# A masked two-layer graph kernel: shorter constant set-up, loads in order of use, four quads ahead of the loop, last units by halves, store wait behind the final branch, and a branch hint

## What is computed

```python
N, D = 4096, 128            # x: (N, D) f32, adj: (N, N) int32, about 0.2% of it ones, diagonal 1
# layer 0, with A' = adj + I: the mask adds nan_to_num(-inf * (1 - A'))
x = layernorm(x + softmax((x @ Wq) @ (x @ Wk).T + mask, axis=1) @ (x @ Wv))
# layer 1
h = x @ W.T + b_W
e = (h @ a1)[:, None] + (h @ a2)[None, :] + b_a[0]
e = where(e > 0, e, 0.2 * e)
att = softmax(where(adj > 0, e, -9e15), axis=1)
x = layernorm(x + att @ h)
```

## Time and profile before

| | us |
|---|---|
| median of 3 runs | 276.06 |
| lowest, highest | 275.21, 276.06 |
| the profiled execution, its own time | 275.45 |
| its span | 273.6 |

### The profile page before, as it was taken

The page is one execution under the profiler, slowest core; times in us unless marked ns, Lnnn a source line. Parts: engine busy times, 40 slices in busy tenths (PEclk is TensorE's granted clock), DMA queues, the critical chain, the costliest instruction groups (busy, mean ns, idle before and its releaser), DMA issues.

```text
span 273.6 us, 3890 instructions
## 1 busy us (share of the span) xinstructions
PE 238.2 (87%) x1488; PEld 133.9 (49%) x1488; DVE 200.6 (73%) x318; ACT 147.5 (54%) x174; POOL 47.8 (17%) x68
## 2 busy tenths in 40 slices
PE   3836599999629999999999999999999999999920
PEld 3734566546224555455644545556555555544410
DVE  2392597999987777877698777786977776978080
ACT  3049864976666557664686676646866750101010
POOL 2065041555540000000022000000220000014020
PEclk9998689999968999999999999999999999999985
DMA  5999999999979999999696989898989100001101
GB/s 146 352 410 403 248 286 419 408 406 351 317 289 320 341 320 340 393 291 412 188 415 180 410 265 401 274 410 257 372 229 415 55 0 0 2 0 38 41 21 61
DMA packets 24057, 71.73 MB, mean 262 GB/s; under 512 B 5347, under 2 KB 5604, under 8 KB 24036
## 3 DMA queue, kind: packets, MB, share of 16 engines
q1 hardware_dynamic: 23748, 71.32, 73.2%
q10 hardware_dynamic: 288, 0.13, 0.2%
HBM read 69.36 MB, written 2.10 MB: 261 GB/s over the span
## 4 chain that ended last, share of the span: by engine, by line
issue 39%; PE 24%; POOL 4%; ACT 1%; DVE 1%; POOLq 0%
PE banks L791 19%; PE banks L771 3%; POOL frstd L330 2%; POOL out_sb L337 2%; PE banks L739 1%; PE banks L819 1%; ACT a L396 1%; DVE e_sb L579 1%; POOLq L236 0%; DVE out_sb L691 0%; ACT R L384 0%; ACT v_exp L372 0%; ACT cr_exp L374 0%; ACT cr_exp L376 0%; DVE frv L604 0%
## 5 line engine op out<-in xcount | busy, mean ns | idle before, releaser
L579 DVE SCALAR_TENSOR_TENSOR e_sb<-R,c_word,banks 128x1024 f32<-128x1024 f32 x128 | 159.5, 1276 | 37.4 <-PE banks L771 36.8
L791 PE MATMUL banks<-e_sb,f_parts 128*128 128x512 f16 x768 | 185.0, 389 | 0.0
L396 ACT ACTIVATE a<-a_sb 128x2048 fp8e4<-128x2048 int32 x64 | 119.8, 1904 | 66.0 <-PE banks L771 51.3
L791 PEld LDWEIGHTS banks<-e_sb,f_parts 128*128 128x128 f16 x768 | 71.8, 97 | 85.4 <-issue 2.2
L771 PEld LDWEIGHTS banks<-ident,a 128*128 128x128 f16 x512 | 34.7, 100 | 15.0 <-DVE e_sb L579 1.0
L771 PE MATMUL banks<-ident,a 128*128 128x128 f16 x512 | 40.1, 223 | 1.0 <-ACT a L396 0.5
L330 POOL TENSOR_TENSOR frstd<-frv,minus_half 128x4 f32<-128x4 f32 x8 | 8.1, 1006 | 169.8 <-DVE frv L604 169.6
L412 ACT ACTIVATE junk<-y 128x128 f32<-128x128 f32 x28 | 8.3, 297 | 22.4 <-DVE y L595 22.4
L724 PE MATMUL banks<-m0c_um,x_tr 128*128 128x130 f32 x64 | 11.2, 336 | 5.0 <-ACT xhat_st L365 5.0
L712 PE MATMUL banks<-ident,x_sb 128*128 128x128 f32 x32 | 6.5, 348 | 8.1 <-DMA x_sb<-in_x_dram 8.1
L739 PE MATMUL banks<-ident,cr_word 128*128 128x128 f32 x32 | 6.3, 330 | 7.8 <-ACT R L384 7.8
(11 more groups left out here) (96 smaller groups left out, 88.2 us busy)
## 6 DMA issues: line engine op xcount, KB each, us to landing
a_sb<-in_adj_dram SPq DMA_DIRECT2D x32, 2048.0 KB, 12.8
x_sb<-in_x_dram SPq DMA_DIRECT2D x8, 256.0 KB, 14.2
out_dram<-out_sb SPq DMA_DIRECT2D x8, 256.0 KB, 6.7
w_nat<-in_L_gnn_W_dram ACTq DMA_DIRECT2D x1, 64.0 KB, 3.3
wv<-in_L_gnn_Wv_dram ACTq DMA_DIRECT2D x1, 64.0 KB, 3.5
acol<-in_L_gnn_a_vec_dram SPq DMA_DIRECT2D x2, 0.5 KB, 3.2
bcol<-in_L_gnn_b_W_dram SPq DMA_DIRECT2D x1, 0.5 KB
brow<-in_L_gnn_b_W_dram SPq DMA_DIRECT2D x1, 0.5 KB
```

The costliest lines, as they stand in the source:

```text
L396: nc.scalar.activation(a8[:, n % 2, Q * h:Q * (h + 1), k * 512:(k + 1) * 512], a_sb[:, a % SLOTS, :].rearrange("p (r n) -> p r n", r=Q) [: ...
L579: nc.vector.scalar_tensor_tensor(out=e_sb[:, k % NE, :], in0=R[:, g % 2, :], scalar=c_word[:, 2 * t + b:2 * t + b + 1], in1=ps_code[s % NA ...
L791: ins = nc.tensor.matmul(ps_acc[g % 2][h][:, :], f[:, j, :], e_half[:, k % NE, cols, part], start=(j == 0 and n == 0), stop=(j == T - 1 an ...
```

## The change

It does nine things:

- **Constants.** A matrix `centre` (I minus 1/D) is made by POOL, so the two centring chains (reduce, scale, subtract on DVE) become matmuls against it. `m0c_um` comes from one matmul of 130 columns (`m0_t` by `centre_u`). The part that only `project` needs moves into `weights2(0)` and `weights2(1)`, behind `layer0(1)` and behind the spreads. `layer0(0)` no longer waits for `cs`, but on DVE the wait for the three bias transfers stands ahead of the copies of `centre_u` and `m0c_um`, and PE's product for `m0c_um` waits for the copy of `centre_u`; `x_turned(1)` and with it ACT's second copy stand behind `weights`.
- **Loads.** Blocks of adj have 512 columns a row (1 MB, runs of 2 KB) in 8 slots instead of 1024 columns (2 MB, runs of 4 KB) in 4. The attention vectors are loaded first, the biases behind the first two blocks.
- **Quads.** Quads 2 and 3 are turned, multiplied and kept ahead of the loop; `x_tr` has 4 buffers. From quad 2 on `divide` is done by POOL.
- **Turns.** `turn(2)` stands behind `sums(0)`, `turn(3)` and `turn(4)` behind `sums(1)`.
- **Spreads** go to slots 11 and 13 of PE; ACT's copies stay in its slots 12 and 14.
- **Group ends** (`ACC_AT` to `VARY_AT`) go one or two slots earlier, and `project` ahead of `turn` in its slot.
- **Last units.** The last three units are summed first for the left half, then for the right; the left half is copied and projected in between; the right half is copied, projected and normalised in two pieces by ACT and DVE.
- **Stores** of groups 0 and 1 are issued between the loads; SP's final wait for the stores moves behind the branch over the general code.
- **Hint.** A branch hint for PE's jump stands behind the last projections.

The core of the diff:

```diff
-    SLOTS = 4
+    LOADS = PARTS * CHUNKS * G
+    SLOTS = 8
-    AHEAD = 3
+    HALVED = 3
-    TURN, COPY, MULTIPLY, KEEP = -9, -7, -7, -5
-    STATS, DIVIDE, EXPS, PACK = -4, -2, -2, -1
-    SPREAD_AT, R_AT = 8, 12
-    ACC_AT, PROJECT_AT, FIN_AT, SQUARE_AT, VARY_AT = 5, 6, 10, 12, 14
+    TURN, COPY, MULTIPLY, KEEP = -8, -7, -6, -5
+    STATS, VARY0, EXPS, PACK = -4, -3, -2, -1
+    SPREAD_AT, R_AT = (11, 13), (12, 14)
+    ACC_AT, PROJECT_AT, FIN_AT, SQUARE_AT, VARY_AT = 4, 5, 8, 10, 12
...
+                def divide(i):
+                    pool.wait_ge(rstd_ready, i + 1)
+                    nc.gpsimd.tensor_tensor(xhat_st[:, quad_tiles(i), :], xhat_st[:, quad_tiles(i), :],
+                                            rstd[:, i % 2, :].unsqueeze(2).broadcast_to([P, Q, D + 2]),
+                                            ALU.mult).then_inc(xhat_later, 1)
...
+                step(nc.vector.tensor_tensor(m0_t[:, :], ps_m0[:, 0:D], ident[:, :], ALU.add))
+                assert done[0] == U_READY
+                dve.wait_ge(biases_loaded, 16 * 3)
...
+                assert done[0] == BB_READY
+                dve.wait_ge(pe_const, 3)
+                step(nc.vector.tensor_copy(centre_u[:, D:D + 2], ps_u[:, 2:4]))
+                dve.wait_ge(pe_const, 4)
+                step(nc.vector.tensor_copy(m0c_um[:, :], ps_m0[:, 0:D + 2]))
+                assert done[0] == M0_READY
...
+                    pe.wait_ge(vec_const, BB_READY + 1)
+                    nc.tensor.matmul(ps_m0[:, 0:D + 2], m0_t[:, :], centre_u[:, :], start=True,
                                      stop=True).then_inc(pe_const, 1)
...
-                    pe.wait_ge(acc_copied, 2 * g + 1)
-                    if last and q == 1:
-                        pe.wait_ge(acc_copied_v, 1)
...
+                def last_sums():
+
+                    units = range(S - HALVED, S)
+                    for s in units:
+                        for b in range(2):
+                            pe.wait_ge(p_ready, 2 * s + b + 1)
+                            ins = products(s, b, 0)
+                    ins.then_inc(half_done, 1)
+                    for s in units:
+                        for b in range(2):
+                            ins = products(s, b, 1)
+                        if s == S - HALVED:
+                            pe.wait_ge(acc_copied, 2 * G - 1)
+                            pe.wait_ge(y_ready, 2 * G - 2)
+                            projections(0, quad(0), range(Q)).then_inc(fin_mm, 1)
+                    ins.then_inc(half_done, 1)
...
+                last_sums()
+                to_end = pe.mark_branch_hint_location()
                 pe.wait_ge(verdict, 13)
...
-                with if_general(pe):
+                before = nc.cur_bb
+                pe.br_cond(pe.value_load(flag[0:1, 0:1]) != 0, "pe_general", "pe_end").branch_hint(to_end)
...
+                for q in range(2):
+                    sp.wait_ge(stored[q], 16 * G)
```

More of the change, by code:

```diff
@@ L221, in graph_layers, with quad_at, wait_xhat @@
         verdict_pe = sem("verdict_pe")
-        def quad_at(slot, offset):
+        def quad_at(slot, offset, first=2):
             i, odd = divmod(slot - offset, 2)
-            return i if not odd and 2 <= i < QUADS else None
+            return i if not odd and first <= i < QUADS else None
+        def wait_xhat(eng, i):
+            if i < 2:
+                eng.wait_ge(xhat_ready, i + 1)
+            else:
+                eng.wait_ge(xhat_later, i - 1)
         def group_at(slot, offset):
@@ L421, in _ @@
                 copy_xt(2)
-                codes(1)
+                copy_xt(3)
                 rows(0, 0, ps_acc[0][0])
                 rows(0, 1, ps_acc[0][1])
+                keep(2)
                 codes(2)
+                keep(3)
                 codes(3)
                 for slot in range(-2, S):
-                    if (i := quad_at(slot, COPY)) is not None and i > 2:
+                    if (i := quad_at(slot, COPY, 4)) is not None:
                         copy_xt(i)
-                    if (i := quad_at(slot, KEEP)) is not None:
+                    if (i := quad_at(slot, KEEP, 4)) is not None:
                         keep(i)
@@ L850, in _ @@
                             project(g, q, quad(2 * (g % 2)))
-                    sums(slot)
-                project(G - 1, 0, quad(0))
-                project(G - 1, 1, quad(4))
+                    if 1 < slot < S - NA:
+                        turn(slot + NA)
+                    if slot < S - HALVED:
+                        sums(slot)
+                    if slot == 0:
+                        turn(2)
+                    elif slot == 1:
+                        turn(3)
+                        turn(4)
+                last_sums()
+                to_end = pe.mark_branch_hint_location()
                 pe.wait_ge(verdict, 13)
@@ new lines, in by_rows, with by_cols @@
+                def by_rows(w):
+                    for i in range(QUADS):
+                        product(nc.tensor.matmul(bank[0][:, :], w[:, :], xhat_t[:, i * QW:(i + 1) * QW],
+                                                 start=True, stop=True))
+                def by_cols(w, bias_row):
+                    for i in range(QUADS):
+                        for q in range(Q):
+                            t = Q * i + q
+                            dst = bank[0][:, q * P:(q + 1) * P]
+                            ins = nc.tensor.matmul(dst, xhat_t[:, t * P:(t + 1) * P], w[:, :], start=True,
+                                                   stop=bias_row is None)
+                            if bias_row is not None:
+                                ins = nc.tensor.matmul(dst, ones[0:1, :], bias_row[:, :], start=False, stop=True)
+                        product(ins)
@@ new lines, in _ @@
+                pe.wait_ge(g_loaded, 64)
+                turned(x_sb)
+                by_rows(wq)
+                by_rows(wk)
+                by_cols(wv, None)
+                tiles(0)
+                turned(xhat)
+                pe.wait_ge(g_small, 1)
+                by_rows(u2_rep)
+                by_cols(w_t, brow)
+                assert made[0] == KEPT[1]
+                for t in range(T):
+                    ins = nc.tensor.matmul(bank[1][:, t:t + 1], xhat_t[:, t * P:(t + 1) * P], u[:, 0:1],
+                                           start=True, stop=True)
@@ L976, in _ @@
+                ins.then_inc(g_made, 1)
+                tiles(1)
+                pe.br("pe_end")
+                nc.switch_bb("pe_end", parent=before)
             @block.scalar
```

491 lines of the change are left out of this document (251 added, 240 removed).

## The result

The median of the changed kernel is 266.73 us (265.68 to 267.30), that of the kernel before on the same chip 275.86: a ratio of 0.967 [0.963, 0.970]. The direction is right; the gain is 9.1 us where 15 were forecast, and the time lies above the range.

A forecast was written before the change was run, and what follows sets the result against it. PE was taken as the bound: its start, one 7.79 us stop and what follows the last sums. 9.6 + 0.2 + 0.3 + 4.9 = 15.0 off 275.45 gave 260.45, as median 261.0 us; range 255.5 to 265.5.

The forecast's parts named there:

- the opening: Set-up until `sums(4)`: the shortened set-up is eaten by biases queued behind adj; +1.1 to -0.6 us, taken as +0.2 us gain.
- The gap and the clock: PE around slot 10: spreads in slots 11 and 13 remove the 7.79 us stop and 1.8 us of half-clock work; 9.6 us.
- from there PE needs 9 slots of 3.15: From the start of `sums(4)` at 50.8 us, PE at its own pace ends `sums(12)` and extras at about 81.4.
- The rival of a new wait in the middle: ACT at its slot 12 or DVE beside busier POOL comes too late, 1 to 2 us each: 263 to 267; chance 0.15.
- `divide` on POOL at no cost: POOL, 16.64 us busy of 33.85, has room for six more operations of 1 us.
- so it is not the bound: Opening: DVE has its first tile of slot 4 about 2 us before `sums(4)`, so DVE does not bound it.
- The rival of early biases: Opening: biases do not queue behind adj and land at about 7, `layer0(0)` 5 us earlier: 256 us; chance 0.1.
- The last units: Kernel end: summing the last units by halves shortens last sums to last store from 15.15 to 14.85 us; 0.3 us.
- Behind the last store: After the last store's issue: earlier meeting and hinted jump cut 7.3 us to 2.4; gain 4.9 us.
- the first rival: PE's jump at the end: the hint does nothing, gain there 1.9 us, total 264.0 us; chance 0.2.
- I take the upper: PE's final jump: of gains 1.9 and 4.9 us, 4.9 chosen, since 5 us precede the jump and the fetch takes 3.8.
- the rival of slow loads: adj loads: rows of 2 KB make DMA the bound; median passes 276 us below 284 GB/s; chance 0.03.

## Why the prediction was right or wrong

**The sum, term by term.** By the forecast's own sum the profiled execution should have had a span of 273.6 - 15.0 = 258.6; it had 265.0. The 6.4 us lie in three places. `sums(4)` starts 2.8 later than before instead of 0.2 earlier: 3.0. From there to `sums(14)` it was 95.81 - 50.78 = 45.03 before and is 89.66 - 53.55 = 36.11 now, 8.9 instead of 9.6: 0.7. From the start of `sums(60)` to the end of the span it was 25.16 and is 23.04, 2.1 instead of 5.2: 3.1. The later groups give back 0.3. Taken alone, the end would have given 264.1 and the opening 264.0, both inside the range; the two together put the time outside.

**The gap and the clock, 9.6: right, 8.9 in the changed kernel.** PE has no wait for `R` in slots 10 to 13: ACT's first copy starts at 80.30, the second spread at 85.62. Taken by itself the move is worth 8.6, taken back out of the change 6.4; the difference is delay that the gap would have swallowed. One step beside the sum failed: "from there PE needs 9 slots of 3.15", from 50.8 to 81.4, 30.6 us. It took 32.1, since from `sums(4)` to `sums(10)` DVE and not PE sets the pace. I had read DVE's room from the earlier trace rows at full pace, where no quad is prepared, and set its pairs of slots at 7.3 to 7.5 us; they took 7.84, 7.61 and 7.84, and DVE had no idle time at all. The rival of a new wait in the middle gave 263 to 267 and so has the measured number, but not its mechanism: there is no stop in slot 13, and the pace accounts for 0.7 us only.

**`divide` on POOL at no cost: wrong.** "POOL had 16.64 busy of 33.85" answered the wrong question: POOL had the time, but its instructions hold up DVE's. Back on DVE the divides were worth 0.4 us of pace in the changed kernel and 1.0 where nothing else was late (0.9 in the median).

**The opening, +0.2: the chain right, one wait missed.** Biases landed at 13.85 (12.9 forecast; 12.7 to 13.9 over the eight profiled executions with this opening), `layer0(0)` at 16.63 (16.1), `keep(2)` done at 31.6 (30.0 to 31.7), `copy_xt(4)` done at 42.0 (40.3 to 42.0). I then added PE's pieces; of DVE I had looked at slot 4 only ("so it is not the bound"). That is the step that failed here. `words(2)` needs `exps(2)`, which stands in ACT's slot 2 behind the same conversions: `sums(4)` at 53.55 against 49.7 to 51.4, 2.8 us later than before. Nor is it enough to take this wait away: the next ones stand right behind it (2.81 us for `keep(4)`, and with early biases 2.82 us for block 8). The biases' place alone costs 3.7 us, more than the whole delay. The forecast had their landing nearly right and let the shortened set-up pay for it; of the 3.0 us by which the opening missed, PE's wait behind `exps(2)` is 1.8, and 0.9 is `copy_xt(4)` at the late end of its range. The rival of early biases was priced too high, since adj then came too late: with them `layer0(0)` started at 10.47, 6.2 us earlier, and 3.7 us and not 5 reached the median.

**The last units, 0.3: right.** From the start of the last sums less a unit to the last store 14.6 us (14.85 forecast, 15.15 before), and 9.03 of them to the end of the sums (9.1).

**Behind the last store, 4.9: wrong, the first rival came.** Of the sum's terms this missed by most. The failed step is "I take the upper, since from the last projections to the jump lie 5 us and the fetch takes 3.8". 3.0 us were counted for the hint, and it took none of the jump away. Without it 1.9 was the figure: 7.3 less 265.0 - 259.3 = 5.7 makes 1.6 here, and the same edit alone, in the kernel before, gave 1.1 to 1.2.

**Rows of 2 KB: the rival of slow loads did not come.** DMA moved 387 GB/s, and 409 with rows of 4 KB, but ACT waited for no block of adj in the changed kernel. With the biases early the small blocks were 2.0 us faster all the same; that this is their arriving in the order of use is read from ACT's first waits, and in the version with 2 MB blocks x stands behind twice as many bytes of adj.

## What to carry to other kernels

Before a stall is taken away, ask which engine was busy without a pause while it lasted: its work, not that of the waiting engine, is the next bound, and it shows no waits. An operation moved to an idle engine is free only if the two engines don't get into each other's way, which the lengths of the small steps beside the new neighbour show. Of many edits try first, alone, the one that removes the longest stall: here it gave nearly the whole gain, and three small transfers queued behind large ones cost 3.7 us, more than the 2.3 that all the others brought together.

## What the runs showed of the hardware

- PE's jump over far code took 3.1 to 3.9 us in fifteen profiles and over near code 0.25 us. A branch hint took it away in none of three forms; why is not shown.
- DVE steps of 0.16 us that begin while a POOL instruction runs can last until its end, up to 1.06 us (L606, 53 to 76 us of the changed kernel); not all do, and `edges`, with one input in PSUM, keep their 1.27 us.
- Three transfers of at most 0.5 KB behind 2 MB of adj had landed at 12.7 to 13.9 us, scattered by 1.2 us from one execution to the next; with only 0.5 MB of x ahead nobody waited for them at 7.24.
- PE's load of the flag took 0.49 us, and 0.64 to 0.75 us beside a store under way.
